# The values of a pair of attention units moved from its second following unit to its first, with new places for all steps

## What is computed

```python
x = L0(x, pos, cond, ...)   # adaptive RMS norm, attention with 8 query heads of 64 and one key/value head,
                            # rotary positions, then an MLP silu(h Wg) * (h Wu) Wd with 2048 inner channels
x = L1(x, cond, mask, ...)  # adaptive layer norm, 16 heads of 32 with normalised q and k, then a gelu MLP of 2048
x = L2(x, cond, ...)        # adaptive layer norm, 16 query heads, 4 key heads through a latent of 128,
                            # rotary positions, block-sparse mask
x = L3(x, cond, ...)        # 8 experts of 64 -> 256 -> 64 channels, layer norm, silu, a 512x512 product
```

```python
scores = einsum('bhqd,bhkd->bhqk', q, k)
p = softmax(scores, axis=-1)
o = einsum('bhqk,bhkd->bhqd', p, v)
```

## Time and profile before

| | us |
|---|---|
| runs of the kernel | 2055.98, 2043.96, 2051.99 |
| median | 2051.99 |
| span of the profiled execution | 2053.7 |
| PE busy in it | 1912.4 (93%) |
| DVE, ACT, POOL busy | 1110.8, 1027.7, 795.9 |
| mean granted clock of PE | 0.960 of full speed |

### The profile page before, as it was taken

How to read it: one execution, slowest core, us unless ns; L and a number is a source line. 1 busy time by engine, 2 the same in 40 slices (tenths; PEclk the granted TensorE clock), 3 DMA queues, 4 the chain that set the end, 5 groups by cost and what they waited for, 6 DMA issues and landing times.

```text
span 2053.7 us, 35242 instructions
## 1 busy us (share of the span) xinstructions
PE 1912.4 (93%) x12880; PEld 1512.5 (74%) x12880; DVE 1110.8 (54%) x3184; ACT 1027.7 (50%) x2474; POOL 795.9 (39%) x1094
## 2 busy tenths in 40 slices
PE   5889999999999999999899989989999989988987
PEld 3567777788888878887778777768876768855565
DVE  5655535644553365345664676574554675366363
ACT  3542423433343344443565465555567565468665
POOL 4556662111124243234667554326332432243230
PEclk9899999999999999999999999989999999989989
DMA  7336677555444534444345433433433335322311
GB/s 249 110 129 209 229 249 264 181 196 190 172 160 177 181 134 171 156 158 153 135 174 187 158 118 139 171 114 107 165 113 134 127 110 195 130 81 69 124 63 52
DMA packets 98795, 314.84 MB, mean 153 GB/s; under 512 B 11584, under 2 KB 13376, under 8 KB 97088
## 3 DMA queue, kind: packets, MB, share of 16 engines
q1 hardware_dynamic: 98624, 312.58, 43.7%
HBM read 242.55 MB, written 66.58 MB: 151 GB/s over the span
## 4 chain that ended last, share of the span: by engine, by line
PE 76%; DVE 10%; POOL 4%; ACT 4%; issue 3%; DMA 1%; SPq 0%; POOLq 0%; DVEq 0%; ACTq 0%
PE B L194 69%; PE B L197 7%; DVE FB L215 2%; POOL R L212 1%; DVE SS L218 1%; DVE T L212 1%; POOL SS L209 1%; ACT SS L200 1%; DVE FB L212 1%; POOL FB L212 1%; DMA ST<-in_wpack 1%; DVE PT L206 1%; ACT FB L200 1%; DVE HA L215 1%; POOL W L212 1%
## 5 line engine op out<-in xcount | busy, mean ns | idle before, releaser
L209 POOL TENSOR_SCALAR SS<-SS,NM 128x256 f32<-128x256 f32 (+1 forms) x640 | 290.2, 471 | 747.3 <-DVE NM L224 747.1
L194 PE MATMUL B<-HM,W 128*128 128x512 f32 x2304 | 540.1, 395 | 9.2 <-DVE HM L215 5.7
L194 PEld LDWEIGHTS B<-HM,W 128*128 128x128 f32 x2304 | 436.5, 190 | 105.6 <-issue 5.0
L194 PE MATMUL B<-G,W 128*128 128x512 f32 x1536 | 391.6, 405 | 8.1 <-POOL W L212 4.3
L194 PEld LDWEIGHTS B<-G,W 128*128 128x128 f32 x1536 | 286.1, 191 | 76.1 <-issue 10.7
L200 ACT ACTIVATE SS<-SS,NM 128x256 f32<-128x256 f32 (+1 forms) x512 | 240.5, 471 | 121.2 <-DVE NM L218 120.8
L194 PE MATMUL B<-HA,W 128*128 128x512 f32 x864 | 229.6, 418 | 6.1 <-DVE HA L212 4.4
L197 PE MATMUL B<-ident,SS 128*128 128x128 f32 x1152 | 180.6, 294 | 41.1 <-POOL SS L209 33.6
L194 PEld LDWEIGHTS B<-HA,W 128*128 128x128 f32 x864 | 170.6, 202 | 45.9 <-issue 5.4
L212 DVE TENSOR_TENSOR G<-FB,G 128x512 fp32r<-128x512 f32 x128 | 99.5, 780 | 165.3 <-ACT G L200 165.2
L197 PEld LDWEIGHTS B<-ident,SS 128*128 128x128 f32 x1152 | 129.9, 147 | 77.6 <-issue 41.1
(11 more groups left out here) (109 smaller groups left out, 2654.0 us busy)
## 6 DMA issues: line engine op xcount, KB each, us to landing
W<-kept SPq DMA_DIRECT2D x357, 512.0 KB, 4.2
kept<-W SPq DMA_DIRECT2D x119, 512.0 KB, 4.6
ST<-in_wpack SPq DMA_DIRECT2D x139, 256.0 KB, 2.9
Y<-in_adaw SPq DMA_DIRECT2D x12, 1024.0 KB, 6.8
FB<-FB SPq DMA_DIRECT2D x52, 64.0 KB, 2.6
X<-in_xT SPq DMA_DIRECT2D x1, 3072.0 KB, 13.0
out_xT<-X SPq DMA_DIRECT2D x12, 256.0 KB, 2.1
FB<-in_pos SPq DMA_DIRECT2D x4, 256.0 KB, 6.0
```

The costliest lines, as they stand in the source:

```text
L194: return self.real.matmul(*a, **k) if self.real is not None else self
L209: return self.real.tensor_scalar(*a, **k) if self.real is not None else self
```

## The change

It touches three things. The step "values" of the pair (g-2, g-1) is now written in unit g with g even, right behind the scores of the pair (g+2, g+3) and ahead of "normalise" of unit g+1. It used to be written in the odd unit g+1, behind "normalise" and ahead of "turn". All halves of the step move with it, on PE, ACT and DVE. LAG becomes 1, since the last pair's values are now due in unit 192. And nearly every number of PLACE is another one; no step is added or dropped.

```diff
@@ Plan.unit
         if a < UNITS and a % 2 == 0:
             self.banks = [self.dp.take() for _ in range(4)]
             self.add("scores", a, self.banks)
+        if g % 2 == 0 and g > 1:
+            self.banked("values", g - 2)
         if 0 <= g + 1 < UNITS:
             self.add("normalise", g + 1)
-        if g % 2 and g > 1:
-            self.banked("values", g - 3)
         if 0 <= g < UNITS:
             us = [self.dp.take() for _ in range(keys(g) * HEADS[layer(g)] // 512)]
             self.add("turn", g, us)
@@ places
-LAG = 2
+LAG = 1
-    "up": [20.361, 37.774, 53.282, 69.2, 84.763, 103.509, 123.675, 150.322],
+    "up": [20.475, 37.774, 53.282, 68.904, 84.763, 103.542, 123.675, 150.322],
-    "m norm": [17.582, 33.706, 50.292, 66.056, 81.912, 97.369, 120.398, 147.186],
-    "m final": [19.712, 35.985, 52.119, 68.347, 84.357, 99.967, 122.714, 149.477],
+    "m norm": [17.309, 33.712, 49.673, 66.451, 81.863, 97.181, 120.127, 147.135],
+    "m final": [19.879, 36.166, 52.119, 68.347, 84.316, 100.389, 122.861, 149.478],
-    "out": [17.616, 33.486, 49.609, 65.605, 81.749, 97.151, 113.474, 129.833, 145.534, 161.755, 177.973, 191.6,
-        194.705],
+        "out": [17.692, 33.652, 49.311, 65.912, 80.808, 97.051, 112.938, 128.586, 145.454, 161.663, 178.069,
+        192.033, 194.574],
-    "z norm": [141.577, 174.923, 183.064, 198.2, 201.446],
+    "z norm": [141.522, 174.619, 183.03, 198.156, 201.178],
-    "q0 first": [-0.458, 0.616],
-    "k0 first": [-0.054, 2.293, 1.626, 3.239],
-    "q0": [-0.46, 1.879, 2.452],
-    "k0": [0.356, 0.84, 1.722, 2.736, 4.534],
-    "v0": [1.914],
+    "q0 first": [-0.804, 0.481],
+    "k0 first": [0.122, 2.674, 1.159, 4.956],
+    "q0": [-1.404, 1.672, 2.16],
+    "k0": [1.243, 0.768, 1.186, 1.889, 4.465],
+    "v0": [1.359],
-    "z stats": [-0.298, -0.298, 0.784, 0.657, 0.657, 1.406, 1.406, 2.27],
+    "z stats": [-0.847, -0.699, 0.124, 0.032, 0.053, 0.782, 0.492, 1.745],
-    "m parts 0": [0, 0.01, 0.02, 0.03],
+    "m parts 0": [0.074, -0.167, 1.043, -0.017],
-    "start": [-12.43, 6, -2.831, -0.049],
-    "ada": [7.843, 21.989, 25.511, 29.324, 31.58, 34.532, 37.145, 40.064, 43.72, 46.196, 49.144],
+    "start": [-12.542, 6.664, -2.92, 1.611],
+    "ada": [6.451, 24.455, 28.895, 31.894, 33.695, 37.041, 39.379, 42.576, 44.834, 48.768, 51.476],
```

More of the change, by code:

```diff
@@ L28 @@
 AHEAD = 2
-LAG = 2
+LAG = 1
 PLACE = {
[6 rows of a table removed]
-    "trig": [3.589, 20.401, 35.517],
-    "out": [17.616, 33.486, 49.609, 65.605, 81.749, 97.151, 113.474, 129.833, 145.534, 161.755, 177.973, 191.6,
-        194.705],
-    "first": [137.43, 169.635, 179.31, 193.854, 198.087],
-    "z norm": [141.577, 174.923, 183.064, 198.2, 201.446],
-    "z final": [144.398, 176.596, 185.493, 204.08, 205.384],
-    "last": [145.545, 178.406, 187.993, 205.459, 209.491],
-    "q0 first": [-0.458, 0.616],
-    "k0 first": [-0.054, 2.293, 1.626, 3.239],
-    "q0": [-0.46, 1.879, 2.452],
-    "k0": [0.356, 0.84, 1.722, 2.736, 4.534],
-    "v0": [1.914],
[L50 to L58, removed]
[4 rows of a table removed]
[L63 to L68, removed]
-    "m parts 0": [0, 0.01, 0.02, 0.03],
-    "down": [0.802],
-    "start": [-12.43, 6, -2.831, -0.049],
-    "ada": [7.843, 21.989, 25.511, 29.324, 31.58, 34.532, 37.145, 40.064, 43.72, 46.196, 49.144],
[6 rows of a table added]
+    "trig": [2.653, 20.26, 35.4],
+        "out": [17.692, 33.652, 49.311, 65.912, 80.808, 97.051, 112.938, 128.586, 145.454, 161.663, 178.069,
+        192.033, 194.574],
+    "first": [137.396, 169.635, 180.055, 193.981, 197.976],
+    "z norm": [141.522, 174.619, 183.03, 198.156, 201.178],
+    "z final": [144.37, 176.951, 185.716, 204.149, 205.997],
+    "last": [145.647, 178.901, 187.993, 205.667, 209.418],
+    "q0 first": [-0.804, 0.481],
[3 more added lines that the diff above has]
+    "v0": [1.359],
+    "q1": [-1.273, 0.368, 1.275],
+    "k1": [0.198, 1.089, 2.211, 2.251, 3.858],
+    "v1": [3.556, 5.071],
+    "q2": [0.14, 1.14],
+    "k2": [-0.355, 1.501, 8.228, 2.203, 2.46],
+    "v2": [2.367],
+    "out 2": [-0.25, -0.2, -0.15, -0.1],
+    "experts": [0.513, 0.533, 2.798, 1.133, 0.603],
+    "experts of one": [-0.012, 0.015, 0.83, 0.836, 0.927],
[4 rows of a table added]
+    "last step": [0.67, 0.659],
+    "a stats": [-0.041, 0.063, 1.292, 1.611, 1.385, 1.782, 1.492, 2.652],
+    "m stats": [0.107, 0.466, 1.051, 0.972, 0.875, 1.187, 1.271, 1.909],
+    "a parts": [2.089, 4.875, 2.482, 0.035],
+    "a parts 0": [1.853, -0.099, -0.078, 0.54],
+    "m parts": [-0.12, -0.208, 0.633, 0.154],
+    "m parts 0": [0.074, -0.167, 1.043, -0.017],
+    "down": [0.796],
+    "start": [-12.542, 6.664, -2.92, 1.611],
+    "ada": [6.451, 24.455, 28.895, 31.894, 33.695, 37.041, 39.379, 42.576, 44.834, 48.768, 51.476],
```

## The result

| | before | after |
|---|---|---|
| median of the runs, us | 2047.97 | 2062.39 |
| lowest and highest of 4 runs | 2042.92, 2055.98 | 2059.06, 2063.36 |
| ratio to before | | 1.0065, 95% interval 1.0037 to 1.0092 |
| profiled execution: time, span | 2055.98, 2053.7 | 2059.06, 2056.9 |
| PE busy, and the rest of the span | 1912.4, 141.3 | 1901.7, 155.2 |

The change made the kernel slower by 0.65%, some 13 us (8 to 19 by the interval). It had been forecast 14 us faster. The two profiles hide most of this: the one of before is of the longest of its four runs, the one of after is of the lowest, so they lie 3.2 us apart.

A forecast was written before the change was run, and what follows sets the result against it. PE, busy 1912.4 of 2053.7 us, was taken as the bound. 2053.7 - 9 - 2 - 1 + 7 - 10 + 1 = 2039.7, less 1.7 from span to median, gave 2038 us; range 2015 to 2070.

The forecast's parts named there:

- The reading of the bound: Whole span: PE bounds; full stretches can't gain, only the start, 900 to 1000 and 1800 to 1900 us can change.
- Part 1: Item 4's output projection: moved ahead of unit 81, shortens the wait for HM, -9 us; CX waits -2 us.
- Part 2: Odd unit's DVE queue: without CX's subtraction the PT copies end sooner, -1 us, bounds 0 and -5.
- Part 3: Even unit: DVE meets the values before the next odd unit's reciprocal, delaying normalising and turn; +7 us of +21 uncovered.
- Part 4: PLACE, whole kernel: the new places shorten waits for T, R and normalising, -10 us; loss bounded at +12.
- Part 5: Places that look worse: swapped keys close to their consumer, +1 us; late last "ada" transpose 0, up to +5.
- The port: Late turns: normalising beside DVE's additions in T takes 2.69 instead of 1.84 us; 7 us worse, 2045 us; chance 0.05.
- The reciprocal behind the values decides: Odd turns with little cover: they wait for the delayed chain, all 21 us unpaid; 2066 us, chance 0.24.
- The forecast's own sign: First 200 us: the turns' waits for POOL's normalising are no more than 13.3 us if the forecast is right.
- Repaid only: Whole kernel: the new places win just what the late reciprocals cost; 2052 us, chance 0.19.

The follow-up runs named there:

- e5: The kernel after with only item 4's output projection put back from 80.808 to 81.749; 2062.62 us, ratio 1.0082 to before.
- e3: The kernel after with the reciprocal and normalising of unit g+1 written ahead of the values; 2052.24 us, ratio 1.0029 to before.
- e17: e1 with layer 0's copies of the values (ACT's copy, DVE's subtraction) kept in the odd unit behind normalise; 2073.77 us, ratio 1.0131 to before.
- e6: e1 with the reciprocal and normalising of unit g+1 written ahead of the values; 2080.39 us, ratio 1.0157 to before.
- e2: The kernel after with the old order of the values and before's output projection places; 2081.86 us, ratio 1.0176 to before.
- e12: The kernel after with layer 0's query projection back at before's offsets; 2087.64 us, ratio 1.0209 to before.
- e7: The kernel after with layer 0's key projection, swaps included, back at before's offsets; 2060.3 us, ratio 1.0064 to before.
- e4: The kernel after with the "ada" modulation products back at before's places; 2069.23 us, ratio 1.0113 to before.
- e1: The kernel before with only the new order of the values, LAG 1 and after's layer 2 output projection offsets; 2084.56 us, ratio 1.0179.
- e16: The kernel before with the values' copies on ACT and DVE moved behind the softmax of the odd unit; 2152.05 us, ratio 1.0508.
- e9: The kernel before with each "ada" weight load written no sooner than the product that the previous load feeds; 2052.02 us, ratio 1.0038.

## Why the prediction was wrong, point by point

The time, 2062.39, lies in the range, but on the other side: forecast 14 us faster, measured 13 us slower. 27 us are to be found.

**The reading of the bound** held in the main. The 400 to 500 us stretch stayed at 99 us of PE in 100. But one loss lies where the forecast looked for none, from 200 to 345 us: 7.2 us of idle time.

**Part 1 (-9) failed, and with it the strongest argument.** "The sum no longer follows the last addition" was right and meant the reverse of what was taken from it: the sums stand at their own places in the list, the first where it was and the others later than before, so HM came no sooner. The bound "0 (the chain begins where it did)" was the answer: in before the last addition and the first sum (954.83) are adjacent in DVE's queue, and I read adjacency as cause. "Its norm stays" was read from the row "m norm" alone; the row "m stats" put its second step behind unit 82. e5 shows no gain from the projection's place, and the wait for HM is 3.83 us, not gone. The granted clock between 980 and 1000 us did rise, from 0.74 to 0.91, but it is 0.91 in e5 too. The 5.2 us had moreover counted PE's idle time as lost to the clock: for 14.3 busy us at 0.74 the estimate is 3.7. The waits for CX fell by 0.9 us in the row shown, not by 2.

**Part 2 (-1)** can't be told: the waits for PT are 5.1 against 5.0 us.

**Part 3 (+7) was right in its mechanism**, as the dense pair of layer 0 shows: CX's subtraction stands before the reciprocal as foretold. Its size fits too, 7.4 us by e3, but with some 7 us of uncertainty, and the 1.7 us for layers 1 and 2 weren't seen by themselves. What was missing: DVE's stand for ACT's copy isn't only the reciprocal's affair. ACT's copy and DVE's subtraction as a whole sit badly in the even unit of layer 0, with before's places for 9.8 us in that layer alone (e17, the reciprocal's part in it), where the reciprocal in all layers is 4.5 (e6). The new order beyond these copies, which part 3 put at nothing as covered, has 9.8 us of idle time in e17 at unit 60, with a held bank.

**Part 4 (-10) failed.** It took the places as an improvement to add to the change's cost. They only repay: with the old order they cost 36 us (e2), with the new one they save 23 of 37. Against before, "the places winning elsewhere" came to less than nothing, because the new places brought 7.2 us of idle time between units 28 and 36, with waits for weights of 7.7 us (before: 4.3) and one of 3.14 for normalising. The forecast had no term for them, though one projection's place is worth 29 us (e12), in good part through such waits. The bound that was set for bad luck, +12, was named from a norm's wait; the size was fair, the place was not. Waits for T, taken as something that the search would reduce, grew by 11.5 us, 9.9 of it after 1700 us (5.1 to 15.0).

**Part 5 (+1)**: nothing is seen of the swapped keys (e7, -0.2). The late "ada" products were harmless too: their old places are 9.8 us worse in after (e4).

**The port**: in the late norm POOL's normalising beside DVE's additions was a rival of 7 us. The sum of the turns' waits after 1700 us went down, from 13.8 to this in after:

```profile
PE B L197 <- POOL SS L209: 7.5, 9, 2.1
```

and of POOL's rows of four multiplications before has two of 2.69 us there, after none of over 2 us; the rows of eight take 4.52 and 3.23 us in before, 4.10 and 3.25 in after. So that rival didn't come about. The Trainium skill, SBUF — State Buffer, section "SBUF: two separate sides", says that a DVE instruction with two SBUF inputs and a POOL instruction that reads SBUF lock each other out of a shared port pair. The 2.69 against 1.84 us agree; no run here tests it by itself.

**The rivals.** "The reciprocal behind the values decides", 2066, is nearest to the time, and half of the 13 us is its mechanism. But its sign in the profile was wrong: it asked for turn waits well above 33.6 us, and they are 25.1. The forecast's own sign, no more than 13.3 us of them in the first 200 us, held (9.5) in a kernel that got slower, so these waits told neither way. That form exists only without the new places (e1, 47.7). "Repaid only", 2052, had the right structure, places against order, and was 10 us short. So after is neither: the places did away with the large turn waits and paid with others (T, weights, and many small ones).

In numbers, of the 27 us: 9 from item 4 (by the wait that stayed), 1 from the CX waits, nothing from part 3, and the remaining 17 from part 4, where -10 should have read about +7. This last is a remainder and wasn't measured, but e3, which takes part 3 away, says the same: it is 5.9 us over before, with the CX waits' 1 us in it.

**Open**: with e17's copies, the order alone still costs 26.8 us (18.6 between the two profiles, 12.0 of it by unit 176). Whether PE's order itself costs isn't known, in layers 1 and 2 and the tail, nor in layer 0 behind the first units, since every run that kept the copies' place also held a bank. And no run isolates which place makes the waits for weights between 230 and 345 us.

## What to carry to other kernels

A schedule of hand-set places and the order of steps inside a unit are one object. A change that moves both can't be costed as the cost of the order less a gain of the places: look for what a single place is tied to (buffers of weights, a queue, the step next to it) and treat new places as worth nothing by themselves. Where two instructions stand next to each other in a timeline, ask which of data, buffer and place holds the second, before counting an earlier first as a gain; the place of the next step in the list, with its offsets, says so without a run. And when a step is moved, ask for each engine's part of it separately: up to unit 16 the matmuls' move cost next to nothing (1.5 us of idle time in e17) and two copies of 0.4 us did not (6.2 in e1). Last, compare two schedules at a unit by PE's idle time and its count of matmuls, not by the time alone.

## What the runs showed of the hardware that was not expected

- Two PSUM evictions of 0.38 and 0.42 us for a pair, written behind the softmax of the same unit, make the kernel 5.1% slower (e16) with ACT busy for 48% of the span and DVE for 52%. Low engine shares don't say that such a move is free; whether the queues or the held bank made it dear is open.
- The same kernel spreads: before runs from 2039.97 to 2055.98 us over all the comparisons here, mostly with its mean granted clock (0.969 in the shortest run, 0.960 in the longest), and its instructions up to about unit 28, the same in e9, took 5.7 us less by unit 24. Single runs of the two kernels, before's 2042.92 to 2055.98 against after's 2059.06 to 2063.36, lie between 3 and 20 us apart.
- A single profile mixes the clock of its execution with the kernel: PE's busy time fell by 10.7 us from before's profile to after's for the same matmuls, with the mean granted clock up from 0.960 to 0.967, and hid most of the 13.9 us of added idle time. For a change of this size the idle time told more than the span.
